# Adding the softmax sums' two bf16 parts with one matmul, and new steps for a chunk's sums, in an attention and FFN kernel on eight cores

## The reference, cut to what matters

```python
def reference(x, Wq, bq, Wk, bk, Wv, bv, Wo, bo, weight, w_scale, bias):
    x = x + _layernorm(_L0_attn_ref(_layernorm(x), ...))   # 16 heads of 128, causal
    x = x + _layernorm(_L0_ffn_ref(_layernorm(x), ...))    # int8 rows times int8 weight
    return x
# attention: x is (4, 4096, 2048) float32
scores = jnp.einsum('bhtd,bhsd->bhts', q, k) * scale
probs = jax.nn.softmax(scores + causal, axis=-1)
y = jnp.einsum('bhts,bhsd->bhtd', probs, v)
```

## Time and profile before

| what | value |
|---|---|
| median of 3 runs | 2188.65 us (2184.33 to 2415.41) |
| the profiled execution's own time | 2185.32 us |
| its span on the slowest core (core 6) | 2183.7 us |
| spans of cores 0, 2, 4, 6 | 2182.1, 2181.4, 2182.0, 2183.7 us |
| spans of cores 1, 3, 5, 7 | 2134.5, 2137.1, 2136.1, 2134.3 us |
| TensorE matmul busy on core 6 | 2071.6 us, 95% of the span |
| VectorE, ScalarE, GpSimd busy on core 6 | 63%, 46%, 12% |
| heads on core 6 | from 382 us to 1578 us, some 75 us each |

### The profile page before, as it was taken

The page is one execution under the profiler, slowest core; times in us unless marked ns, Lnnn a source line. Parts: engine busy times, 40 slices in busy tenths (PEclk is TensorE's granted clock), DMA queues, the critical chain, the costliest instruction groups (busy, mean ns, idle before and its releaser), DMA issues.

```text
span 2183.7 us, 35313 instructions; the slowest of 8 cores (2134.3 to 2183.7 us)
## 1 busy us (share of the span) xinstructions
PE 2071.6 (95%) x11038; PEld 970.4 (44%) x11252; DVE 1380.1 (63%) x2403; ACT 1002.4 (46%) x1438; POOL 256.0 (12%) x444
## 2 busy tenths in 40 slices
PE   5999999999999999999999999998999999999997
PEld 3444444444444444444444444444344444444443
DVE  5722312576676677667767666766577777776676
ACT  5820000556555655655565556555633333333332
POOL 1100100011011101101110111023001111111111
PEclk9999999999999999999999999999999999999999
DMA  8942121121122022202211220256333333333322
GB/s 294 323 96 66 42 65 39 31 41 27 25 42 42 10 43 43 40 11 43 41 26 25 44 42 10 43 103 167 130 138 116 116 114 108 116 116 116 102 97 74
DMA packets 167392, 172.87 MB, mean 79 GB/s; under 512 B 135842, under 2 KB 146594, under 8 KB 157474
## 3 DMA queue, kind: packets, MB, share of 16 engines
q1 hardware_dynamic: 158564, 132.77, 19.7%
q0 software_dynamic: 8640, 37.75, 8.3%
HBM read 140.61 MB, written 44.04 MB: 85 GB/s over the span
## 4 chain that ended last, share of the span: by engine, by line
PE 81%; DVE 8%; issue 5%; ACT 3%; DMA 2%; DVEq 0%; SPq 0%; POOL 0%; ACTq 0%; POOLq 0%
PE ps L743 22%; PE ps L918 12%; PE ps L902 11%; PE ps L730 11%; PE ps L778 9%; PE ps L795 8%; PE ps L809 3%; DVE rb L1203 2%; DVE rb L1201 1%; DMA xin<-x_seq 1%; PE ps L837 1%; ACT xln L939 1%; ACT P L985 1%; PE ps L819 1%; DVE lo L1191 1%
## 5 line engine op out<-in xcount | busy, mean ns | idle before, releaser
L985 ACT ACTIVATE P<-ps,negb 128x512 bf16<-128x512 f32 (+2 forms) x1104 | 678.6, 618 | 476.4 <-PE ps L778 465.2
L743 PE MATMUL ps<-xT,wqk 128*128 128x384 bf16 (+1 forms) x2997 | 736.0, 352 | 3.5
L743 PEld LDWEIGHTS ps<-xT,wqk 128*128 128x128 bf16 x3072 | 296.8, 98 | 258.8 <-issue 2.3
L778 PE MATMUL ps<-kq 128*128 128x512 bf16 (+2 forms) x1086 | 376.5, 347 | 11.9 <-ACT P L985 10.1
L795 PE MATMUL ps<-P,v_sb 128*128 128x512 bf16 (+3 forms) x1072 | 367.3, 345 | 20.6 <-DVE P L1181 19.0
L730 PE MATMUL ps<-wv,xT 128*128 128x512 bf16 x1313 | 292.2, 380 | 1.7 <-issue 0.2
L918 PE MATMUL ps<-xT,qx 128*128 128x512 bf16 x1317 | 291.8, 379 | 1.4
L902 PE MATMUL ps<-xT,yj 128*128 128x512 bf16 x1191 | 273.2, 379 | 1.3
L918 PEld LDWEIGHTS ps<-xT,qx 128*128 128x128 bf16 x1344 | 131.5, 98 | 158.6
L730 PEld LDWEIGHTS ps<-wv,xT 128*128 128x128 bf16 x1344 | 131.0, 98 | 155.0 <-issue 2.5
L1134 DVE TENSOR_SCALAR kq<-ps,bqk 128x384 bf16<-128x384 f32 (+1 forms) x192 | 131.1, 683 | 87.6 <-PE ps L743 84.6
(11 more groups left out here) (96 smaller groups left out, 1721.1 us busy)
## 6 DMA issues: line engine op xcount, KB each, us to landing
xin<-x_seq SPq DMA_DIRECT2D x21, 1024.0 KB, 9.0
x<-x_seq SPq DMA_DIRECT2D x21, 1024.0 KB, 4.9
out<-x SPq DMA_DIRECT2D x20, 1024.0 KB, 3.8
v_g<-vst SPq DMA_DIRECT2D x84, 128.0 KB, 1.8
v_sb<-v_g SPq DMA_DIRECT2D x16, 672.0 KB, 5.0
yj<-yt_h SPq DMA_DIRECT2D x21, 512.0 KB, 5.7
stage<-wv_p SPq DMA_DIRECT2D x8, 1024.0 KB, 9.8
wqk<-wq_p POOLq DMA_DIRECT2D x16, 512.0 KB, 5.2
```

The costliest lines, as they stand in the source:

```text
L743: mm = pe.matmul(ps[:, JOB + job % 2, 0:n * 128], wqk[p][:, 0 if kind == "q" else 1, kc, :], xt_cols(pl, a, n, kc), start=(kc == 0), stop= ...
L778: pe.matmul(ps[:, S_BANK + s % 2, q0 * 128:n * 128], k_cols(pl, h, kt, 1), q_cols(pl, h, a + q0, n - q0), start=True, stop=True).then_inc( ...
L985: a.activation(P[:, s % RP, q0 * 128:m], ps[:, S_BANK + s % 2, q0 * 128:m], AF.Exp, bias=negb[:, k:k + 1], scale=SCALE).then_inc(S["exp_ok ...
```

## The change

It does four things.

1. `hi` and `lo` become one buffer. `row1` is a column that is 1 in the second row of each group of 32 and 0 elsewhere, `row01` one that is 1 in the first and the second. VectorE writes `hi` = sums times `row1` (zero in the first row), then `hilo` = sums times `row01` less `hi`, which leaves bf16(sums) in the first row of a group, the remainder in the second and zeros in the others. `combine` is then one matmul with plain ones over the 32 or 128 rows of `hilo`.
2. The steps of the splits and combines are written into the plan. In the first plan the combines of c2, c3 and c4 move from 24, 37, 54 to 25, 38, 55, that of c5 from step 6 of the next head to step 9; the sums of c1 move from step 11 to 13 and the copy of its values from 12 to 14. The rule for `bound_at` is as before, but with these steps it puts the bound of the next head's first query chunk at step 30 in place of 11, and that of the first round of keys at 32 in place of 29. In the last head c5 is still combined at 6 steps after the head's end. In the second plan no step moves.
3. Behind the last head, the output projection's third tile waits in its third bank for the copy of the last chunk's values, no longer for their product.
4. There too, VectorE takes the third tile's statistics ahead of the second tile's quantisation, no longer behind its scale.

```diff
-        self.late = [2 if len(ks) < 6 else 0 for ks in self.keys]
...
+        self.late = [2 if len(ks) <= 6 else 0 for ks in self.keys]
+        self.split_at, self.comb_at = splits, combs
...
-         [[5, 4, 3], [0, 1, 2]], True, 30),
+         [[5, 4, 3], [0, 1, 2]], [6, 14, 21, 34, 51, 72], 30,
+         [10, 15, 21, 34, 51, 72], [14, 19, 25, 38, 55, 78]),
...
             def combine(h, c):
-                sel = sel1 if pl.groups[c] == 1 else sel4
-                m = 128 * pl.queries[c][1]
+                r, m = 32 * pl.groups[c], 128 * pl.queries[c][1]
                 w.wait_ge("lo_ok", h * NC + c + 1)
                 open_misc("comb", h, c)
-                pe.matmul(ps[:, MISC, 0:m], sel[:, :], hi[:, 0:m], start=True, stop=False)
-                pe.matmul(ps[:, MISC, 0:m], sel[:, :], lo[:, 0:m], start=False, stop=True
+                pe.matmul(ps[:, MISC, 0:m], ones[0:r, :], hilo[0:r, 0:m], start=True, stop=True
...
-                            w.wait_ge("y_ev", H * NC)
+                            w.wait_ge("yc_ok" if pl.copies else "y_ev", H * NC)
...
-                v.tensor_copy(hi[0:r, 0:m], ps[0:r, DEN, 0:m]).then_inc(S["hi_ok"], 1)
+                v.tensor_scalar(hi[0:r, 0:m], ps[0:r, DEN, 0:m], row1[0:r, :], None, ALU.mult
+                                ).then_inc(S["hi_ok"], 1)
                 w.wait_ge("hi_ok", n + 1)
-                v.tensor_tensor(lo[0:r, 0:m], ps[0:r, DEN, 0:m], hi[0:r, 0:m], ALU.subtract
-                                ).then_inc(S["lo_ok"], 1)
+                v.scalar_tensor_tensor(hilo[0:r, 0:m], ps[0:r, DEN, 0:m], row01[0:r, :],
+                                       hi[0:r, 0:m], ALU.mult, ALU.subtract
+                                       ).then_inc(S["lo_ok"], 1)
...
-            quant_scale(1)
             i = 4
             for j in range(2, NQ):
                 w.wait_ge("nm_c", i)
-                norm_of(ps[:, 0:4, :].rearrange("p a b -> p (a b)"), i, "c", ("o_mm", 4 * j + 1))
+                norm_stats(ps[:, 0:4, :].rearrange("p a b -> p (a b)"), i, "c",
+                           ("o_mm", 4 * j + 1))
                 if j == 2:
+                    quant_scale(1)
                     quant_out(1)
+                norm_scalars(i, "c")
```

More of the change, by code:

```diff
@@ L32, with __init__ @@
 class Plan:
-    def __init__(self, tiles, chunks, queries, jobs, rounds, copies, o_from):
+    def __init__(self, tiles, chunks, queries, jobs, rounds, copies, o_from, splits, combs):
         self.tiles, self.chunks, self.queries, self.jobs = tiles, chunks, queries, jobs
@@ L107, in __init__ @@
                      for j in range(self.NJ)]
-        self.late = [2 if len(ks) < 6 else 0 for ks in self.keys]
-        self.split_at, self.comb_at = [], []
-        last = LAG + 6
+        self.late = [2 if len(ks) <= 6 else 0 for ks in self.keys]
+        self.split_at, self.comb_at = splits, combs
         for c in range(self.NC):
-            end = self.first[c + 1] - 1
-            self.split_at.append(max(end + LAG + 1 + self.late[c], last + 1))
-            self.comb_at.append(max(self.split_at[-1] + 3, last + 5))
-            last = self.comb_at[-1]
+            assert splits[c] > self.first[c + 1] - 1 + LAG + self.late[c]
+            assert combs[c] > splits[c] > (combs[c - 1] if c else combs[-1] - self.N)
         taken = {(x + d) % self.N for x in self.comb_at for d in (-2, -1, 0, 1, 2, 3)}
@@ L165, in comb_due @@
     def comb_due(self, g):
+        if g >= H * self.N:
+            return (H - 1, self.NC - 1) if g == H * self.N + LAG + 3 else None
         for h in (g // self.N, g // self.N - 1):
@@ L192, in copy_due @@
         for h in (g // self.N, g // self.N - 1):
-            i = g - h * self.N - LAG
-            if self.copies and 0 <= h < H and i in self.first[1:]:
-                return h, self.first.index(i) - 1
+            i = g - h * self.N
+            if self.copies and 0 <= h < H and i in self.copies:
+                return h, self.copies.index(i)
         return None
@@ L235 @@
 KQ = max(p.NK + p.NQ for p in PLANS) * 128
[L238 removed]
+SEMS = (["id_in", "const_in", "cst", "rw_ok", "wqk0", "wqk1"]
         + ["wv%d%d" % (s, k) for s in range(2) for k in range(4)] + ["bv%d" % g for g in range(NG)]
@@ L356, in build_nc @@
         hi = at("hi", [128, 512], BF16, A + 48 * KB)
-        lo = at("lo", [128, 512], BF16, A + 49 * KB)
+        hilo = at("hilo", [128, 512], BF16, A + 49 * KB)
         P = at("P", [128, RP, 512], BF16, A + 50 * KB)
@@ L1048, in vector_program @@
             v.memset(ones[:, :], 1.0)
-            v.memset(sel1[:, :], 0.0)
+            v.memset(row1[:, :], 0.0)
+            v.memset(row01[:, :], 0.0)
             v.memset(sel2[:, :], 0.0)
-            v.memset(sel4[:, :], 0.0)
             v.memset(half[:, :], 0.5)
@@ L1058, in vector_program, with norm_moments @@
             w.wait_ge("bo_a", 2)
+            v.memset(sel2[0:1, :], 1.0)
+            v.memset(sel2[32:33, :], 1.0)
             for q in range(4):
-                if q < 1:
-                    v.memset(sel1[32 * q:32 * q + 1, :], 1.0)
-                if q < 2:
-                    v.memset(sel2[32 * q:32 * q + 1, :], 1.0)
-                last = v.memset(sel4[32 * q:32 * q + 1, :], 1.0)
+                v.memset(row01[32 * q:32 * q + 2, :], 1.0)
+                last = v.memset(row1[32 * q:32 * q + 2, :], 1.0)
+            last.then_inc(S["rw_ok"], 1)
+            w.wait_ge("rw_ok", 1)
+            for q in range(4):
+                last = v.memset(row1[32 * q:32 * q + 1, :], 0.0)
             last.then_inc(S["cst"], 1)
             stats = {"c": 0}
-            def norm_end(parts, i, tag):
+            def norm_moments(parts, i, tag):
                 if i >= 1:
@@ L1072, in norm_end, with norm_scalars @@
                 v.bn_aggr(mv[:, :], parts[:, :, :]).then_inc(S["ag_" + tag], 1)
+            def norm_scalars(i, tag):
                 w.wait_ge("sd_" + tag, i + 1)
@@ L1078, in norm_end, with norm_stats @@
                                 ALU.mult, ALU.mult).then_inc(S["nm_" + tag], 1)
-            def norm_of(src, i, tag, waits=None):
+            def norm_end(parts, i, tag):
+                norm_moments(parts, i, tag)
+                norm_scalars(i, tag)
+            def norm_stats(src, i, tag, waits=None):
                 for k in range(4):
@@ L1087, in norm_of @@
                 w.wait_ge("bn_" + tag, stats[tag])
-                norm_end(bn6, i, tag)
+                norm_moments(bn6, i, tag)
+            def norm_of(src, i, tag, waits=None):
+                norm_stats(src, i, tag, waits)
+                norm_scalars(i, tag)
             def x_begin(t):
@@ L1244, in vector_program @@
             v.memset(hi[:, :], 0.0)
-            v.memset(lo[:, :], 0.0)
+            v.memset(hilo[:, :], 0.0)
             for t in range(V2_AT):
```

5 lines of the change are left out of this document (2 added, 3 removed), and 3 rows, old and new, of the table PLANS.

## The result

| what | before | after |
|---|---|---|
| median, both on the same chip | 2188.16 us | 2176.97 us (2172.63 at the lowest) |
| ratio of the times | | 0.995 (95% interval 0.9937 to 0.9962) |
| spans of cores 0, 2, 4, 6 | 2182.1, 2181.4, 2182.0, 2183.7 | 2168.8, 2167.5, 2175.4, 2173.1 |
| spans of cores 1, 3, 5, 7 | 2134.3 to 2137.1 | 2128.6 to 2132.4 |

A forecast was written before the change was run, and what follows sets the result against it. The even cores' TensorE, 95% busy, bounds the kernel, with VectorE's chain setting steps 9 to 19 of a head. Heads 12.0, last head 4.5 and end 0.5 sum to 17.0 us off 2185.3: 2168 us, range 2148 to 2184.

The forecast's parts named there:

- the likeliest case: The forecast itself, 2168 us: VectorE's chain sets the stretch and removed waits come back elsewhere; chance 0.62.
- Matmuls removed: Second matmul of each combine pair gone in 16 heads: 17.8 us of TensorE work, 9.3 on the second plan.
- Split instructions: The two split instructions on VectorE: multiplication by a column +0.09 us, subtraction +0.05, together +0.14 a split.
- The chain: VectorE's list from c5's combine to step 16's mask, 12.3 us, sets that stretch's end; gain only 0.11 us.
- c2, c3, c4: Rest of a head: c2 gains 0.56 us, c3 and c4 0.42, against a wait of some 0.3 after c4's combine.
- Mask waits: Sign of being right: the TensorE's waits for masks grow from 19 to over 30 us.
- Last head: Step 8's mask done before c5's reciprocals: 3.3 us of at most 4.7; with c2 and three matmuls, 4.5 gained.
- Behind the last head: After the last head the 2.1 us product wait goes, the 2.3 us ScalarE wait mostly stays: 0.5 us gained.
- the waits really go: Rival: VectorE's chain ends before the TensorE needs it, 2129 us, chance 0.05; about half of it, 2148, chance 0.13.
- all comes back: Rival: chain costs 0.5 us a head more, c4's wait doubles, head gain 0; 2180 us, chance 0.15.
- The slower case: Rival: VectorE's chain, starting three steps later and longer than reckoned, decides every head; 2193 us, chance 0.05.
- the Trainium skill's rule: c0's 32-row combine at step 14 may drain the array; the TensorE waits there anyhow, so the sum is unchanged.

The follow-up runs named there:

- e1: Changed kernel with the first plan's old split and combine steps, keeping one buffer and one combine matmul: 2180.49 us, ratio 0.9972.
- e3: Changed kernel with items 3 and 4 of the change, at the end, taken back: 2175.75 us, ratio 0.9932.
- e6: Changed kernel with combines of c5 at step 6, c0 13, c1 18, c4 54, c1's split 14, output projection's fill from step 35: 2147.73 us, ratio 0.9819.
- e9: e6 with item 3 taken back, so the third bank waits for the last chunk's product again: 2145.06 us, ratio 0.9797.
- e4: Changed kernel with the output projection's fill from step 35 of the last head in place of 30: 2171.67 us, ratio 0.9916.
- e10: e6 with item 4 taken back, so the second tile's scale precedes the third tile's statistics again: 2147.45 us, ratio 0.9811.
- e5: Changed kernel with c5's combine alone back at step 6 of the next head in place of step 9: 2165.05 us, ratio 0.9899.

## Why the prediction was right, and where it was wrong

The time lay within the range, 9 us above the number, and the likeliest case, VectorE's chain in place of the waits removed, is what happened. That the total came so near is in part luck: the heads gave 3.6 us more than forecast, the last head and what follows 7.2 us less. By its steps:

- **Matmuls removed:** right; 95 recorded combines on core 6 where one of its 96 is missing from the trace. On the odd cores 0.50 of their 0.58 us a head counts.
- **Split instructions.** The subtraction was sized rightly (617 and 750 ns). The multiplication's mean is 565 ns for 384 columns, where the copy took 523 and 616 was taken from the projection's row. But both means mix two places: behind a reciprocal (c1) the copy took 494 ns and the multiplication 518, behind a product (c2) 550 and 612 (core 2). So the column costs 0.02 or 0.06 us, and c0's and c1's split together took 1.15 + 1.16 us where 1.26 + 1.21 were reckoned. The Trainium skill (VectorE: DVE Perf Modes, the section on the TRN2 errata) gives 525 ns, an estimate by its formula, whatever the scalar. The copy's 523 ns, which seemed to bear it out, is the mean of 494 and 550, and for 512 columns the copy's 692 ns lies above the formula's 658, an estimate too.
- **The chain:** forecast 12.32 us from c5's combine to the values that wait for the mask of step 16, measured 12.14; no instruction in it waits for the TensorE, and the waits that took the place of the old ones are the forecast ones (c0's combine, the masks of steps 15 and 16). Gain up to step 20 0.36 us, of which 0.17 is the bound's matmul, moved to step 30 and paid there (steps 29 to 37 take 8.54 in place of 8.37): 0.2 net, against 0.11. What the prediction says of the stretch before, almost no gap on VectorE, does not hold: VectorE waited there 1.27 us for c0's combine.
- **c2, c3, c4:** steps 20 to 29 gained 0.70 (forecast 0.56), steps 37 to 60 gained 0.44 (0.42 for c3 and c4); behind step 60, 0.23 came back at line 769 (0.3). A head gains 1.10 in head 9 and 1.04 in the mean over fifteen (15.6 / 15), against 0.8: 15.6 us in place of 12.0.
- **Mask waits** did not grow to over 30 us but to 25.8. Forecast were 2.7 us of waits a head; on core 6 they are 1.62 for masks and some 0.34 at c0's combine (on core 2 that one is shown as issue time), 2.0 in all. So the TensorE's own way over the chain's 12.14 us is 10.1 us, not the 9.6 of the forecast. This changes no time, since VectorE sets the end.
- **Last head: the step that failed.** "I take 3.3 ... with c2's 0.56 and three matmuls of 0.21: 4.5" came out at -1.0. The 4.73 us of the earlier trace rows did go, and by step 12 the head was 6.6 us ahead (1.5 of them because c1's sums and a wait of 0.9 us for the split now come behind step 12). At step 20 2.8 us were left, at step 31 it was 0.4 behind. Three things took the lead, and the prediction has a term for none of them. First, the mask of step 8 did not take 1.90 us for standing behind the reciprocals. In each trace read for this (the even cores of before, of the change, of e1, e3 to e6 and of e9) one mask alone takes over 0.5 us, and it ends 0.08 us behind an instruction of GpSimd, which prepares the output projection's bias in that stretch. Before the change that is

```profile
1520.11 2.16 POOL L688 CAST bohl<-bof 1x2048 bf16<-1x2048 f32 x1
```

beside the mask of the earlier trace rows, and now the mask of step 15, which takes 0.21 us in head 9:

```profile
1506.12 4.32 POOL L694 TENSOR_TENSOR bohl<-bof,bhi 1x2048 bf16<-1x2048 f32 x1
...
1509.06 1.47 DVE L1196 TENSOR_TENSOR P<-P,tri 128x128 bf16<-128x128 bf16 x1
```

  So this cost did not go but fell on another mask. With c5's product before it (1.45 us in place of 0.69) it had made up some 2.4 of the 4.73 us, by estimate. Now product and mask of step 15 take 1.18 and 1.47 us, and the wait at step 18 is 1.94 us in place of 1.01; no run moved GpSimd's work. Second, between steps 12 and 20 the clock was at half for 8.2 us, before for 4.6. Third, at step 30 the load of attention rows, whose time is not set by the TensorE, took the 2.7 us that were left, and the 3.4 us at half clock behind that wait another 0.9 (steps 31 to 35 take 4.38 us in place of 3.45). Before the change there was a wait of 1.32 us for the same load. The question not asked was what the TensorE meets next when it comes earlier. 5.5 us of the total are missing for this; e4, without the third, brings the last head to 63.2 us, 3.0 better than before.
- **Behind the last head:** forecast +0.5, measured -1.3 on core 2 and -1.4 to -2.4 on cores 0, 4 and 6. The waits fell about as forecast, from 4.3 us in two to 3.7 to 3.9 in one. What the forecast had no term for is the clock: behind the one wait all four even cores run 3.4 or 6.8 us at half of it, and none did before. e9 puts item 3 at a loss of 0.2 to 2.0 us by core, e10 item 4 at a gain of 0.5 us of wait.
- **The rest of the 9 us.** Core 4, not core 6, ended last: its fifteen heads took 1116.8 us where core 2's took 1112.0. It had three stretches of 3.4 us at half the clock in them, at 1.7 us each, where core 2 had none; before, it had one. Its last head and its end took 2.9 us more than core 2's. The time of before beside this run was also 2.8 us above its profiled execution, as the prediction had allowed.

The rivals: that the waits really go is refuted by the mask waits; that all comes back is refuted by heads of 74.05. The slower case's mechanism, the chain starting three steps later, was real and cost 0.8 us a head, as e5 shows. It was covered by what the other steps gave. The prediction treated the chain's start as fixed by the plan and asked only how long it is; whether it should start at step 6 or 9 was the larger question, worth 12 us.

On the Trainium skill's rule (TensorEngine Tiling (Array Packing), Key Properties) that a change of tiling mode drains the array: the rows fit it. The matmul after c0's combine over 32 rows starts 0.25 us behind it (1062.66 to 1062.91), where 384 columns take 0.16, so 0.09 us later. The combine stands in a place where the TensorE waits for VectorE in any case, so the rule decides nothing here, as forecast.

## What to carry to other kernels

When one engine's unbroken list sets a stretch, count instructions there and look at where the list starts, before counting what another engine saves: here 0.7 us more on the list cost 0.7 us, and its start three steps earlier gave 0.8, while three matmuls saved in the same steps, with longer splits, gave 0.16. Clearing an instruction out of another's way is bought with its later start, so try each move alone; the change as a whole was faster although one of its moves was a loss. And where a stage is made to arrive earlier, look at the first thing it meets that is not timed by it, a transfer above all: at a last head or a stage's border the gain is gone there, and here, starting the consumer five steps later brought 4 us back. And where one instruction takes far longer than its like, look at what the other engines do until it ends, before its place in the order is blamed.

## What the runs showed of the hardware that was not expected

**Half clock in the last head.** In the last head the granted clock is 0.52 over 14 us after the change (the row at e4), with the TensorE busy 10.6 us of them; before, over the matching stretch, it is 0.66:

```profile
1521.00:1535.00 14.00, 10.01 (x43) 3.61 (x44) 9.92 (x15) 6.56 (x13) 5.32 (x2) 0.66 1.04 424
```

0.5 is the lower of the two levels, 1.2 GHz. It fell to it 11.0 us into the head, and before the change 12.1 us into it. What the TensorE did ahead of that: after the change no wait of over a microsecond, but five for ScalarE (0.15 to 0.58 us) and one of 0.92 for the split of c0, with the TensorE busy 4.65 of the last 6.8 us; before, the wait of 4.73 us for the mask, in which it fell. Core 4 of the changed kernel also has a stretch of 3.4 us in the midst of head 9 (granted clock 0.83 from 1070 to 1080 us), where the TensorE is otherwise at the full level, and where before the same core had none. Its heads have the same waits as core 2's, which shows no such stretch there. Why one core falls and another not stays open. In sum an even core spent 21 to 28 us at half clock before, 31 to 48 after and 25 to 29 in e6, whose waits for masks are shorter; each is worth half its length at most.

**A mask held until GpSimd is through.** The rows under the last head: a 128x128 mask on VectorE that takes 0.2 us elsewhere took 1.47 or 1.90 us beside a GpSimd instruction, and ended 0.08 us behind it, on every even core and in every run read for it. A product of 128x512 beside another took 1.18 us in place of 0.69.

**What stands ahead of a VectorE instruction is part of its time.** Reading PSUM with 384 columns and 32 rows, the multiplication by a column took 506 ns behind a reciprocal (the changed kernel) and 599 ns behind a mask (e1). So the column is priced only between rows of the same place: 518 against 494 ns behind a reciprocal, 612 against 550 behind a product (128 rows), and with 512 columns 750 against 692.
